# A quarter of the mask matmuls becomes a capped minimum on VectorE, in a two-layer decoder on one Trainium2 core

## The reference: what is computed

```python
scores = jnp.where(attn_mask[None, None, :, :], -jnp.inf, scores)
```

## Time and profile before

| what | value |
|---|---|
| median of 3 runs | 895.78 us (891.18 to 896.17) |
| the profiled execution's own time | 894.7 us |
| its span, first to last instruction | 892.9 us |
| mean granted TensorE clock | 0.941 of 2.4 GHz |
| busy: PE, DVE, ACT, POOL | 776.4, 656.8, 479.7, 356.8 us |

### The profile page before, as it was taken

The page is one execution under the profiler, slowest core; times in us unless marked ns, Lnnn a source line. Parts: engine busy times, 40 slices in busy tenths (PEclk is TensorE's granted clock), DMA queues, the critical chain, the costliest instruction groups (busy, mean ns, idle before and its releaser), DMA issues.

```text
span 892.9 us, 18862 instructions
## 1 busy us (share of the span) xinstructions
PE 776.4 (87%) x6106; PEld 421.5 (47%) x6106; DVE 656.8 (74%) x2253; ACT 479.7 (54%) x998; POOL 356.8 (40%) x904
## 2 busy tenths in 40 slices
PE   1688599999999888978899999999999988968865
PEld 0346334443445545546465544555544544543444
DVE  6568767878888876867788888987898867557331
ACT  3423256564656456656556665467655754834623
POOL 8875102121234443445465322245333434443134
PEclk9779799999999899999999999999999998988967
DMA  9698903011304465534827422144325153054000
GB/s 297 142 184 202 167 9 58 9 51 33 80 21 102 104 137 107 114 59 81 182 67 137 102 51 56 38 101 95 82 59 98 48 112 78 12 120 69 2 0 12
DMA packets 123810, 77.70 MB, mean 87 GB/s; under 512 B 8184, under 2 KB 122048, under 8 KB 123584
## 3 DMA queue, kind: packets, MB, share of 16 engines
q1 hardware_dynamic: 123712, 76.50, 39.9%
HBM read 41.90 MB, written 32.90 MB: 84 GB/s over the span
## 4 chain that ended last, share of the span: by engine, by line
PE 60%; DVE 14%; DMA 7%; issue 6%; ACT 5%; POOL 5%; SPq 3%; DVEq 0%; POOLq 0%; ACTq 0%
PE ob L1297 10%; PE mb L1245 8%; PE eb L1273 5%; PE eb L1274 5%; PE side L1165 3%; PE side L1156 3%; PE side L1173 3%; DMA QP<-bounce 2%; PE eb L1277 2%; PE eb L1268 2%; DMA QW<-bounce 2%; PE side L1092 2%; PE eb L1270 2%; ACT probs L1481 2%; DVE junk L1758 2%
## 5 line engine op out<-in xcount | busy, mean ns | idle before, releaser
L1481 ACT ACTIVATE probs<-eb 128x512 f32<-128x512 f32 (+1 forms) x512 | 274.3, 568 | 197.4 <-PE eb L1274 103.4
L1758 DVE CUSTOM_DVE_ANT_0 junk<-mb,maskq_add 128x512 bf16<-128x512 f32 x256 | 169.5, 689 | 41.2 <-PE mb L1245 36.2
L1297 PE MATMUL ob<-probs,V 128*32 128x256 f32 (+1 forms) x2048 | 130.4, 372 | 2.2 <-ACT probs L1481 2.1
L1063 POOL TENSOR_SCALAR nm<-mx 128x8 bf16<-128x8 f32 x80 | 19.9, 248 | 238.5 <-DVE mx L1758 132.8
L1273 PE MATMUL eb<-maskk_add,identb 128*128 128x512 bf16 x256 | 98.1, 383 | 7.8 <-issue 6.4
L1766 DVE TENSOR_REDUCE mx<-mb 128x1 f32<-128x512 f32 x128 | 83.4, 686 | 28.1 <-PE mb L1245 26.6
L1245 PE MATMUL mb<-KS,QP 128*128 128x512 bf16 x256 | 91.1, 391 | 9.6 <-DVE mx L1758 6.3
L1274 PE MATMUL eb<-QP,KS 128*128 128x512 bf16 x256 | 97.8, 382 | 0.0
L967 POOL TENSOR_SCALAR rstd<-mv 128x2 f32<-128x2 f32 x64 | 16.6, 259 | 178.1 <-DVE mv L1544 176.9
L1297 PEld LDWEIGHTS ob<-probs,V 128*32 128x32 f32 x2048 | 54.6, 109 | 59.5 <-issue 30.4
L1245 PE MATMUL mb<-KS,QW 112*128 112x512 bf16 x128 | 49.3, 420 | 12.4 <-DVE mx L1766 8.0
(11 more groups left out here) (196 smaller groups left out, 1592.7 us busy)
## 6 DMA issues: line engine op xcount, KB each, us to landing
QP<-bounce SPq DMA_DIRECT2D x48, 256.0 KB, 5.6
KS<-bounce SPq DMA_DIRECT2D x32, 384.0 KB, 7.0
bounce<-scratch SPq DMA_DIRECT2D x48, 192.0 KB, 2.3
bounce<-scratch SPq DMA_DIRECT2D x64, 128.0 KB, 2.1
KS<-bounce SPq DMA_DIRECT2D x32, 192.0 KB, 4.2
bounce<-scratch SPq DMA_DIRECT2D x16, 384.0 KB, 2.6
bounce<-scratch SPq DMA_DIRECT2D x16, 256.0 KB, 3.0
bounce<-scratch SPq DMA_DIRECT2D x48, 64.0 KB, 1.8
```

The source lines that it names most:

```text
L1297: ins = nc.tensor.matmul(bank[32 * j:32 * j + 32, S - n:S], v_of(core, kt, 4 * g + j), pr[:, (j % 2) * n:(j % 2 + 1) * n], start=(first_ a ...
L1481: nc.scalar.activation(probs[:, u % PROBS, 0:n], eb[:, u % 2, 0:n], ACT.Exp, scale=SCALE[core.p]).then_inc(probs_by[1], 1)
L1758: ins = V_.tensor_tensor_reduce(junk[:, e.n % 2, :], bank, maskq_add[:, t, :], 1.0, NEG_EXP, ALU.add, ALU.max, mx[slot][:, t, h:h + 1])
```

## The change

Of phase 1 the units 0 and 4 of each group, and of phase 2 unit 0, no longer get the mask matmul. ScalarE takes the exponential of the unmasked scores, and VectorE then takes the smaller of each probability and a cap, 0 where the key is masked and 3e38 elsewhere, in place in `probs`. The value products of phases 1 and 2 wait for that. Two cap tables are made at the start, one context buffer is given up, and the planner gets a kind of work "cap" with a price of 0.62 us and new ranks and shifts.

```diff
+CAP = 3.0e38
-LANES, SLOTS, WIDES, OUTS, OB, QN, MROWS, CTXS = 3, 3, 2, 3, 1, 3, 4, 6
+LANES, SLOTS, WIDES, OUTS, OB, QN, MROWS, CTXS = 3, 3, 2, 3, 1, 3, 4, 5
+CAPPED, CAP_DVE = ((1, 0), (1, 4), (2, 0)), 0.62
-URGENT = {("end", 2): 1, ("end", 4): 2, ("to0", 3): 3, ("to1", 1): 3, ("to1", 6): 1, ("to1", 7): -1, ("to3", 5): 3}
-LATER = {("end", 2): 2, ("end", 4): 3, ("end", 5): 3, ("to0", 3): 2, ("to0", 6): -2, ("to0", 7): 2, ("to1", 1): 2, ("to1", 5): 1, ("to1", 7): -3}
-AFTER = {(2, 0): -1, (2, 4): 2, (2, 7): -2, (3, 2): 3, (3, 7): 1}
-RANK = {"turn": -1, "nm": 0, "row": -1, "chain": 0.8, "keep": 0.5, "chain on TensorE": 2.8, "max": 3.0, "exp": 3, "av": 4}
+URGENT = {("end", 2): 1, ("end", 3): 2, ("end", 4): 2, ("end", 6): 2, ("to0", 3): 3, ("to1", 1): 3, ("to1", 4): 3, ("to1", 7): -1, ("to2", 3): 3,
+    ("to3", 4): 2, ("to3", 5): 3}
+LATER = {("end", 0): 3, ("end", 2): 2, ("end", 4): 3, ("end", 5): 3, ("to0", 3): 2, ("to0", 6): -2, ("to0", 7): 2, ("to1", 0): -2, ("to1", 1): 2,
+    ("to1", 5): 1, ("to1", 7): -3, ("to2", 5): 3, ("to3", 2): -3}
+AFTER = {(1, 0): -1, (1, 4): 2, (1, 6): 2, (2, 0): -1, (2, 4): 2, (2, 7): -2, (3, 1): 3, (3, 2): 3, (3, 4): -2, (3, 6): -2, (3, 7): -2}
+RANK = {"turn": -1, "nm": 0, "row": -1, "chain": 0, "keep": 0.5, "chain on TensorE": 0.3, "cap": 1, "max": 0.6, "exp": 3, "av": 4}
...
+            if e == "dve" and cap_queue and exp_made[cap_queue[0].n] <= t:
+                found.append((RANK["cap"], 0, "cap", None, cap_queue[0]))
...
-                us = SHORT_PE if core.p == 2 and ev.i >= 2 else EXP_PE[core.p]
+                us = SHORT_PE if core.p == 2 and ev.i >= 2 or (core.p, ev.i) in CAPPED else EXP_PE[core.p]
...
+        mask_cap = sb("mask_cap", [P, 2, S], BF16)
+        window_cap = sb("window_cap", [P, 2, P], BF16)
...
+                link(G.memset(window_cap[:], CAP))
                 for i, sign in ((0, 1), (1, -1)):
                     select(wink_add[:, i, :], ALU.is_ge, NEG_MAX, [[sign, P]], -sign)
+                    select(window_cap[:, i, :], ALU.is_ge, 0.0, [[sign, P]], -sign)
...
-                    nc.tensor.matmul(part, identb[:], wink_add[:].rearrange("p a q -> p (a q)")[:, 0:n].unsqueeze(1).to_broadcast([P, 2, n]),
-                                     start=True, stop=False, skip_group_check=True)
-                    ins = nc.tensor.matmul(part, k_of(core, h, kt * P, P), q_of(core, h, 2)[:, :, S - n:S], start=False, stop=True, skip_group_check=True)
+                    if i:
+                        nc.tensor.matmul(part, identb[:], wink_add[:].rearrange("p a q -> p (a q)")[:, 0:n].unsqueeze(1).to_broadcast([P, 2, n]),
+                                         start=True, stop=False, skip_group_check=True)
+                    ins = nc.tensor.matmul(part, k_of(core, h, kt * P, P), q_of(core, h, 2)[:, :, S - n:S], start=(i == 0), stop=True, skip_group_check=True)
...
+                    if i % 4:
+                        nc.tensor.matmul(part, identb[:], maskk_add[:, kt:kt + 1, :].to_broadcast([P, 2, S]), start=True, stop=False, skip_group_check=True)
+                    ins = nc.tensor.matmul(part, k_of(core, h, kt * P, P), q_of(core, h, 2), start=(i % 4 == 0), stop=True, skip_group_check=True)
...
                 pe.wait_ge(probs_by[MADE_BY[u + QUAD - 1]], MADE[u + QUAD - 1])
+                if core.p in (1, 2):
+                    pe.wait_ge(capped, CAP_TO[u])
...
                 nc.scalar.activation(maskq_add[:], maskq8, ACT.Copy, scale=NEG_MAX)
+                nc.scalar.activation(mask_cap[:], maskk8[:, 0::2, :], ACT.Copy, bias=CAP, scale=-CAP)
...
+            def capped_probs(e):
+
+                dve.wait_ge(probs_by[1], MADE[e.n])
+                if e.core.p == 1:
+                    dve.wait_ge(masks_ready, 1)
+                    cap = mask_cap[:, e.i // 4:e.i // 4 + 1, :].to_broadcast([P, 2, S])
+                else:
+                    cap = window_cap[:].rearrange("p a q -> p (a q)").unsqueeze(1).to_broadcast([P, 2, S])
+                pr = probs[:, e.n % PROBS, :].rearrange("p (j q) -> p j q", j=2)
+                V_.tensor_tensor(pr, pr, cap, ALU.min).then_inc(capped, 1)
```

More of the change, by code:

```diff
@@ L70 @@
 X_LAND, W_LANDS, ROWS_LAND = (3.2, 5.6, 7.5, 17.0, 17.7, 18.4, 19.1, 19.8), 5.2, 10.5
-CTX_LAND, CTX_LANDS = (20.5, 21.2, 21.9, 22.6, 23.3, 24.0), 6.0
+CTX_LAND, CTX_LANDS = (20.5, 21.2, 21.9, 22.6, 23.3), 6.0
 TERNARY = 10
@@ L214, in plan @@
     exp_queue, av_queue, keep_queue = [], [], []
+    cap_queue, capped = [], {}
     max_core = exp_core = None
@@ L314, in plan @@
                     a = av_queue[0]
-                    if exp_made[QUAD * a.n + QUAD - 1] <= t and (not a.first or a.turn < OB or (a.turn - OB < len(keep_done) and keep_done[a.turn - OB] <= t)):
+                    if exp_made[QUAD * a.n + QUAD - 1] <= t and (a.core.p in (0, 3) or capped.get(QUAD * a.n, never) <= t) and (not a.first or a.turn < OB or (a.turn - OB < len(keep_done) and keep_done[a.turn - OB] <= t)):
                         found.append((RANK["av"], 0, "av", None, a))
@@ L412, in plan @@
                 ev.core.nm[ev.g] = t + NM_POOL + SEEN
+            elif kind == "cap":
+                ev = cap_queue.pop(0)
+                order[e].append((t, ev))
+                free[e] = t + CAP_DVE - LEAVES[e]
+                capped[ev.n] = t + CAP_DVE + SEEN
             elif kind == "row":
@@ L443, in plan @@
                 exp_made[ev.n] = t + us + SEEN
+                if (ev.core.p, ev.i) in CAPPED:
+                    cap_queue.append(Event("cap", ev.core, ev.g, ev.i, ev.n))
             elif kind == "av":
@@ L494 @@
 NM_N = {(e.core, e.g): i for i, e in enumerate([e for _, e in ORDER["pool"] if e.kind == "nm"])}
+CAP_TO = {e.n: i + 1 for i, e in enumerate([e for _, e in ORDER["dve"] if e.kind == "cap"])}
 MROW_DMAS = (0, 2, 2, 4)
@@ L689, in decoder @@
         max_scores, max_used, nm_ready = sem("max_scores"), sem("max_used"), sem("nm_ready")
-        exp_scores, av_done, out_kept = sem("exp_scores"), sem("av_done"), sem("out_kept")
+        exp_scores, capped, av_done, out_kept = sem("exp_scores"), sem("capped"), sem("av_done"), sem("out_kept")
         probs_by = (sem("probs_by_dve"), sem("probs_by_act"))
@@ L1267, in scores @@
                     part = bank[:, 0:2 * n].rearrange("p (j q) -> p j q", j=2)
-                    nc.tensor.matmul(part, identb[:], wink_add[:].rearrange("p a q -> p (a q)")[:, 0:n].unsqueeze(1).to_broadcast([P, 2, n]),
-                                     start=True, stop=False, skip_group_check=True)
-                    ins = nc.tensor.matmul(part, k_of(core, h, kt * P, P), q_of(core, h, 2)[:, :, S - n:S], start=False, stop=True, skip_group_check=True)
+                    if i:
+                        nc.tensor.matmul(part, identb[:], wink_add[:].rearrange("p a q -> p (a q)")[:, 0:n].unsqueeze(1).to_broadcast([P, 2, n]),
+                                         start=True, stop=False, skip_group_check=True)
+                    ins = nc.tensor.matmul(part, k_of(core, h, kt * P, P), q_of(core, h, 2)[:, :, S - n:S], start=(i == 0), stop=True, skip_group_check=True)
                 elif p == 1:
                     part = bank.rearrange("p (j q) -> p j q", j=2)
-                    nc.tensor.matmul(part, identb[:], maskk_add[:, kt:kt + 1, :].to_broadcast([P, 2, S]), start=True, stop=False, skip_group_check=True)
-                    ins = nc.tensor.matmul(part, k_of(core, h, kt * P, P), q_of(core, h, 2), start=False, stop=True, skip_group_check=True)
+                    if i % 4:
+                        nc.tensor.matmul(part, identb[:], maskk_add[:, kt:kt + 1, :].to_broadcast([P, 2, S]), start=True, stop=False, skip_group_check=True)
+                    ins = nc.tensor.matmul(part, k_of(core, h, kt * P, P), q_of(core, h, 2), start=(i % 4 == 0), stop=True, skip_group_check=True)
                 else:
@@ L1783, in _ @@
             prelude.update({f"queries {i}": partial(clear_queries, i) for i in range(SLOTS)})
-            in_plan("dve", prelude, {"max": maxima, "turn": maxima, "exp": masked_products}, chain_steps)
+            in_plan("dve", prelude, {"cap": capped_probs, "max": maxima, "turn": maxima, "exp": masked_products}, chain_steps)
 def in_order(w, heads):
```

## The result

The changed kernel takes 917.72 us (median of 4, 913.52 to 918.63) against 895.97 us for the kernel before: a ratio of 1.0252, 95% interval 1.0215 to 1.029. It is 22 us slower where 10 us faster was forecast, and lies above the range. Times in this document are medians of all runs; the ratios leave out two runs, one of each kernel with halved maxima, that were more than 1.5% above the fastest of their kernel.

The account below looks back on a forecast made before the run. TensorE was taken as the bound, with VectorE some 15% behind. Gains of 5.8 and 5.6 us less 1.6 and 0.3 us paid made 9.5 us off 894.7 us, so 885 us; range 866 to 904.

Parts of the forecast that it names:

- TensorE is full.: From 150 to 300 and 500 to 700 us, TensorE was read as busy 145.8 of 150 and 196.3 of 200 us.
- Direct gain: 96 mask matmuls leaving TensorE, by their shares of the chain: 17.3 us, bounds 0 and 20.6 us.
- The price of a cap: Each of 96 minima on VectorE takes 0.74 us, GpSimd contention included: 71 us in all, ends 59 and 80 us.
- Does VectorE hide it? I take half.: Caps just fit VectorE's free time in the two full stretches: 5.8 of 11.7 us gained there, all 5.6 us elsewhere.
- The new waits: At value products waiting for caps: a sixth of 96 caps late by 0.1 us, 1.6 us paid, ends 0 and 29.
- The start and the contexts: Cap tables made at the start and one context buffer fewer: 0.3 us paid, ends -0.5 and 2.
- The new order: New ranks and shifts across all streams: taken as 0, with 13 us as both ends.
- VectorE becomes the bound: Rival: caps wait behind maxima in VectorE's stream and TensorE stands at the value products: 906 us, chance 0.20.
- What would show it: Expected signs: L1273 at 192, L1268 at 96, caps' mean 0.65 to 0.83 us, VectorE above 95% in full stretches, TensorE's sum down 36 us.

Follow-up runs that it names:

- the control: Kernel before, same order and all mask matmuls, no caps, but both cap tables made at the start and five context buffers: 892.19 us, 1.001.
- the searched one: Ranks and shifts from a random search over the planner's tables: 894.95 us with the change's work, 887.49 without caps and masks, 890.77 with before's work.
- the run without caps: Order of the kernel before, a quarter of the mask matmuls gone, caps and the waits for them left out: 890.15 us, 0.9961.
- the old order with caps: Order of the kernel before, a quarter of the mask matmuls gone, each cap put into VectorE's stream behind its exponential: 915.86 us, 1.0239.

## Why the prediction was wrong, step by step

- **"TensorE is full."** Wrong reading. 97% busy counts each matmul to its modelled end, 0.38 us, where the next starts after 0.215 us. The forms in that stretch of the kernel before, by busy us and mean ns:

```profile
L1273 PE MATMUL eb<-maskk_add,identb 128*128 128x512 bf16 x92 | 35.0, 381 | 1.4 <-ACT probs L1481 1.0
L1274 PE MATMUL eb<-QP,KS 128*128 128x512 bf16 x92 | 34.9, 379 | 0.0
L1297 PE MATMUL ob<-probs,V 128*32 128x256 f32 x432 | 29.6, 386 | 1.0 <-ACT probs L1481 0.8
L1245 PE MATMUL mb<-KS,QP 128*128 128x512 bf16 x71 | 24.4, 383 | 1.0 <-DVE mx L1758 0.8
```

  The first, second and fourth are 255 x 0.215 = 55 us in steps, for 94 us shown. Summing all forms of the stretch so (value products at 1.00 us for 16, f32 products at their own steps) gives, as an estimate, some 133 of 150 us: about 17 us of holes, not 4. A change that removes TensorE's work then partly widens holes: the loads' wait for the banks of maxima is 48.5 us with the 96 matmuls out and 41.6 us in the control.
- **Direct gain, 17.3 us, of which 11.4 us were counted.** This term failed. The shares of the chain say what the end waited for, not what it would do without it: the 96 matmuls are worth 4 us in the old order, 14 in the change's, 3 in the searched one, each with 5 or 6 us to either side.
- **The price of a cap, 0.74 us and 71 us in all.** Right within 6%: means 0.687 and 0.727 us, 67.1 us. The figure from the two-SBUF-sided row, scaled by a column's price (0.682 us), met the median (0.685 us).
- **"Does VectorE hide it? I take half."** This step failed, and it is the one that turns the sign. It compared caps with VectorE's free time in a stretch, and even so counted a gain of 5.8 us in the two full stretches; against the run without caps, the profiled execution of the old order with caps lost 26 us there. A free microsecond in a fixed stream is not free if the next maximum is waited for. In the old order some 44% of the time held came through with the first cap (21 of 48.6 us), all of it with the second.
- **The new waits, 1.6 us.** About right: 0.4% with caps of one column, which the noise does not tell from none, and 1.5 us of TensorE's idle time at the value products.
- **The start and the contexts, 0.3 us.** Right within what the control can tell.
- **The new order, 0 with 13 us on both sides.** This step failed: with before's work it costs 20 us (1.0232 for 1.001, some 7 us to either side), with the matmuls out and no caps 10 us (1.0076 for 0.9961). Taking 0 for a replaced order was a guess where the trace had nothing to offer, and the ends should have been wider. In the kernel as changed, on top of the caps, it costs next to nothing more. What in the order costs the time stays open; its lower granted clock is a candidate.
- **The rivals.** "VectorE becomes the bound" came nearest, with 906 us for 918 measured, but by another path: I priced TensorE's wait at the value products, which stayed at 1.5 us, and not its wait for the banks of maxima, which was in my own rows as the longest between the two engines. It priced no new order either.
- **What would show it.** The counts of L1273 and L1268 and the caps' mean came out. VectorE above 95% in the full stretches did not: 131.3 of 150 and 169.5 of 200 us after the change, 88 and 85%. VectorE sets the pace without being full. TensorE's 36 us less in modelled durations did not come either: its busy time counts overlapping durations once, and without the 96 matmuls it is 764.8 for 776.4 us.

## What to carry to other kernels

Before moving work from a busy engine to a less busy one, look at what the second engine releases: caps in front of maxima delayed the engine that was to be relieved, though VectorE stood at 74%. In a kernel whose order is written by hand, measure a change of work in the old order and the new order with the old work; here either alone showed the loss, and only the table of both showed that the swap was seen to pay in none of the orders run. A chain's share was here an upper bound in all three orders; leaving the instructions out, as the runs without masks did, tells what they are worth.

## What was not expected of the hardware

GpSimd pays for the caps too. The first step of its negation of maxima, in the old order with caps of one column, with full caps and with each cap done twice:

```profile
L1084 POOL TENSOR_SCALAR nm<-mx 128x8 bf16<-128x8 f32 x80 | 19.9, 249 | 241.1 <-DVE mx L1795 134.8 <-DVE mx L1799 55.3 <-DVE mx L1803 50.7
```

```profile
L1084 POOL TENSOR_SCALAR nm<-mx 128x8 bf16<-128x8 f32 x80 | 21.6, 270 | 248.5 <-DVE mx L1795 140.7 <-DVE mx L1799 55.6 <-DVE mx L1803 51.9
```

```profile
L1084 POOL TENSOR_SCALAR nm<-mx 128x8 bf16<-128x8 f32 x80 | 22.7, 283 | 287.1 <-DVE mx L1796 162.3 <-DVE mx L1800 66.9 <-DVE mx L1804 57.6
```

And in the change's order, with before's work and after the change:

```profile
L1082 POOL TENSOR_SCALAR nm<-mx 128x8 bf16<-128x8 f32 x80 | 19.8, 248 | 271.5 <-DVE mx L1791 163.3 <-DVE mx L1799 57.9 <-DVE mx L1795 50.1
```

```profile
L1082 POOL TENSOR_SCALAR nm<-mx 128x8 bf16<-128x8 f32 x80 | 24.8, 310 | 265.2 <-DVE mx L1793 158.9 <-DVE mx L1801 56.3 <-DVE mx L1797 49.8
```

The same instruction takes 249, 270 and 283 ns on average in the old order, 248 and 310 ns in the change's. GpSimd's busy time in the old order is 357.1 us without caps, 356.8 with caps of one column, 371.8 with one full cap and 388.1 with two, some 15 us for each set; the waits alone, which the small caps keep, cost it nothing. The full caps' own medians are 0.684 and 0.686 us there, and their means 0.703 and 0.791 us put some 4.5 us, an estimate, on VectorE's side. I had priced the collision on VectorE's side alone. The Trainium skill, SBUF — State Buffer, section Who interferes with whom, says that a VectorE instruction with two SBUF inputs contends with GpSimd's reads and that the later one waits; the traces agree that the two engines slow each other, and show that here GpSimd pays the larger part.

The granted clock goes with the order of the work: in all four runs of the changed kernel its mean is 0.926 to 0.932, in the profiled run of before 0.941, and 0.941 to 0.950 in the old order with caps. The largest fall against before is in the stretch from 550 to 600 us (0.86, for 1.00 before), where ScalarE is busy 20.4 of 50 us.
